# Router scores of a transformer layer: 32 small matmul groups moved from the normalisation loop to one batch behind it

## The reference

```python
xn = _layernorm(x, axis=-1)
x = x + attn(xn, Wq, Wk, Wv, Wo) + ffn(xn, router_w, bias, gate_w, up_w, down_w, sh_gate_w, sh_up_w, sh_down_w)
...
q = split_heads(x @ Wq.T); k = ...; v = ...          # 16 heads of 64
z = softmax(einsum('byq,byk->bkq', q, k) / sqrt(64))  # 64x64 per head, summed over the 4096 tokens
z = merge_heads(einsum('byz,bvy->bvz', z, v)) @ Wo.T
...
scores = sigmoid(x_flat @ router_w.T)                 # 16 experts
# best 2 of 4 groups, best 4 experts in them, weights normalised and times 2.5
routed = einsum('td,te->td', silu(x@gate)*(x@up) @ down, combine)
out = routed + shared experts (2 x 1024 wide)
```

## Time and profile before

| what | us |
|---|---|
| median of 2 runs (7301.42 to 7302.06) | 7301.74 |
| the profiled execution | 7300.52 |
| its span on the slowest core, core 7 | 7298.8 |
| spans of all cores | 7285.4 to 7298.8 |
| stage one, start of the span to the start of the softmax | 735.1 |

### The profile page before, as it was taken

How to read it: one execution, slowest core, us unless ns; L and a number is a source line. 1 busy time by engine, 2 the same in 40 slices (tenths; PEclk the granted TensorE clock), 3 DMA queues, 4 the chain that set the end, 5 groups by cost and what they waited for, 6 DMA issues and landing times.

```text
span 7298.8 us, 72612 instructions; the slowest of 8 cores (7285.4 to 7298.8 us)
## 1 busy us (share of the span) xinstructions
PE 6570.1 (90%) x30272; PEld 2954.1 (40%) x30272; DVE 1913.1 (26%) x3003; ACT 1469.9 (20%) x1905; POOL 170.6 (2%) x195
## 2 busy tenths in 40 slices
PE   1445777999999999999999999999999999999998
PEld 0222223444444444444444444444444444444443
DVE  1222442222222222222222222222222222222222
ACT  1110001222222222222222222222222222222221
POOL 0000000000000000000000000000000000000000
PEclk9778888999999999999999999999999999999999
DMA  5320222223222222222232432222222222222223
GB/s 100 62 48 22 72 92 55 46 35 45 37 42 40 35 35 35 35 35 35 35 45 37 67 55 42 37 45 35 35 35 35 35 35 35 41 41 40 42 36 57
DMA packets 275598, 323.53 MB, mean 44 GB/s; under 512 B 72496, under 2 KB 215856, under 8 KB 275280
## 3 DMA queue, kind: packets, MB, share of 16 engines
q0 software_dynamic: 193536, 251.70, 23.0%
q1 hardware_dynamic: 81744, 67.20, 3.5%
HBM read 503.42 MB, written 33.55 MB: 74 GB/s over the span
## 4 chain that ended last, share of the span: by engine, by line
PE 84%; DVE 3%; DMA 2%; issue 1%; DVEq 0%; SPq 0%; ACT 0%; POOLq 0%; POOL 0%; ACTq 0%
PE pheap L878 14%; PE pheap L808 14%; PE pheap L804 14%; PE pheap L881 14%; PE pheap L770 14%; PE pheap L774 14%; PE pheap L607 1%; DMA heap<-x 1%; DVE heap L817 1%; DVE heap L820 1%; DVE heap L631 1%; PE pheap L662 0%; DMA heap<-upw 0%; DVE heap L674 0%; DMA out<-heap 0%
## 5 line engine op out<-in xcount | busy, mean ns | idle before, releaser
L878 PE MATMUL pheap<-heap 128*128 128x512 bf16 x4608 | 1746.1, 379 | 124.1 <-DVE heap L820 124.1
L770 PE MATMUL pheap<-heap 128*128 128x512 bf16 x4608 | 1747.2, 379 | 29.8 <-DMA heap<-gatew 29.8
L783 ACT ACT_TABLE_LOAD x576 | 739.0, 1283 | 5137.1 <-PE pheap L774 5118.3
L804 PE MATMUL pheap<-heap 128*128 128x512 bf16 x4608 | 1748.8, 380 | 22.1 <-DVE heap L820 14.4
L808 PE MATMUL pheap<-heap 128*128 128x512 bf16 x4608 | 1748.7, 379 | 0.0
L774 PE MATMUL pheap<-heap 128*128 128x512 bf16 x4608 | 1747.2, 379 | 0.0
L881 PE MATMUL pheap<-heap 128*128 128x512 bf16 x4608 | 1746.2, 379 | 0.0
L817 DVE TENSOR_TENSOR heap<-pheap,heap 128x512 bf16<-128x512 f32 x576 | 398.4, 692 | 3244.1 <-PE pheap L808 3244.1
L902 DVE SCALAR_TENSOR_TENSOR heap<-pheap,heap 128x512 f32<-128x512 f32 x576 | 428.9, 745 | 1322.9 <-PE pheap L881 1322.9
L878 PEld LDWEIGHTS pheap<-heap 128*128 128x128 bf16 x4608 | 450.5, 98 | 692.8 <-issue 157.5
L770 PEld LDWEIGHTS pheap<-heap 128*128 128x128 bf16 x4608 | 451.1, 98 | 574.2 <-issue 31.1
(11 more groups left out here) (88 smaller groups left out, 1238.0 us busy)
## 6 DMA issues: line engine op xcount, KB each, us to landing
heap<-downw POOLq DMA_DIRECT2D x32, 2048.0 KB, 16.2
heap<-gatew POOLq DMA_DIRECT2D x62, 1024.0 KB, 11.3
heap<-upw POOLq DMA_DIRECT2D x62, 1024.0 KB, 15.7
heap<-x SPq DMA_DIRECT2D x64, 512.0 KB, 4.3
out<-heap SPq DMA_DIRECT2D x32, 512.0 KB, 2.9
out<-heap POOLq DMA_DIRECT2D x8, 2048.0 KB, 14.9
heap<-shg POOLq DMA_DIRECT2D x8, 1024.0 KB, 11.2
heap<-shu POOLq DMA_DIRECT2D x8, 1024.0 KB, 15.4
```

The costliest lines, as they stand in the source:

```text
L770: mm = t.matmul(bankf(0, 512), lhs, xnT[:, c * T + h * HALF + sa * 512: c * T + h * HALF + (sa + 1) * 512], start=(c == 0), stop=(c == 7))
L783: a = sc.activation(gfb[:, :], bankf(0, 512), AF.Silu, bias=f32(0.0), scale=f32(1.0))
L804: mm = t.matmul(bankf(1, 512), lhs, xnT[:, c * T + h * HALF + sa * 512: c * T + h * HALF + (sa + 1) * 512], start=(c == 0), stop=(c == 7))
L878: mm = t.matmul(bankf(bpar, 512), lhs, dwb[:, ft * D: ft * D + 512], start=(ft == 0), stop=(ft == 7))
```

## The change

The per-tile router work leaves the loop. Behind the last `emit_qk` a new loop over the tiles computes the 16 dot products of each tile, now in two PSUM banks in turn (3 and 7), and VectorE copies each 128x16 result into one 128x512 SBUF tile (`p3_em`). One Exp, one add and one reciprocal over the whole 128x512 follow. The buffers `p3_em`, `p3_tmp` and `p3_r16` belong to the routing decision and lie where the `x` tiles lay. `SCORES_DONE` is now the count after that reciprocal.

```diff
-                def p12_mm(t, i=i, par=par, sxtp=sxtp):
-                    sxtp.wait_at(t, rt_at[i])
-                    if i == 0:
-                        swt.wait_at(t, WQ_SWT)
-                    if i > 0:
-                        ssig.wait_at(t, score_at[i - 1])
-                    mm = None
-                    for c in range(8):
-                        mm = t.matmul(bankf(3, 16), xnT[:, c * T + i * P: c * T + (i + 1) * P],
-                                      rwT[:, c * 16:(c + 1) * 16],
-                                      start=(c == 0), stop=(c == 7))
-                    stt.inc(mm, 1)
-                block.tensor(p12_mm)
-
-                def p12_s3(sc, i=i):
-                    stt.wait(sc)
-                    if i > 0:
-                        sv.wait_at(sc, sxe_at[i - 1])
-                    ssig.inc(sc.activation(escore[:, :], bankf(3, 16),
-                                           AF.Exp, bias=f32(0.0), scale=f32(-1.0)), 1)
-                block.scalar(p12_s3)
-                score_at[i] = ssig.v
-
-                def p12_v3(v, i=i):
-                    ssig.wait_at(v, score_at[i])
-                    v.tensor_scalar(escore[:, :], escore[:, :], 1.0, None, ALU.add)
-                    v.drain()
-                    sv.inc(v.reciprocal(scores[:, 16 * i:16 * i + 16], escore[:, :]), 1)
-                block.vector(p12_v3)
-                sxe_at[i] = sv.v
...
             for k in range(NT - LAG, NT):
                 emit_qk(k)
+
+            for i in range(NT):
+                rb = 3 if i % 2 == 0 else 7
+
+                def p12_mm(t, i=i, rb=rb):
+                    if i == 0:
+                        sxt0.wait(t)
+                        sxt1.wait(t)
+                        swt.wait_at(t, WQ_SWT)
+                    if i >= 2:
+                        ssig.wait_at(t, ssig.v - 1)
+                    mm = None
+                    for c in range(8):
+                        mm = t.matmul(bankf(rb, 16), xnT[:, c * T + i * P: c * T + (i + 1) * P],
+                                      rwT[:, c * 16:(c + 1) * 16],
+                                      start=(c == 0), stop=(c == 7))
+                    stt.inc(mm, 1)
+                block.tensor(p12_mm)
+
+                def p12_lc(v, i=i, rb=rb):
+                    stt.wait(v)
+                    ssig.inc(v.tensor_copy(p3_em[:, 16 * i:16 * i + 16], bankf(rb, 16)), 1)
+                block.vector(p12_lc)
+
+            def p12_sexp(sc):
+                ssig.wait(sc)
+                ssc.inc(sc.activation(p3_tmp[:, 0:NT * 16], p3_em[:, 0:NT * 16],
+                                      AF.Exp, bias=f32(0.0), scale=f32(-1.0)), 1)
+            block.scalar(p12_sexp)
+
+            def p12_srec(v):
+                ssc.wait(v)
+                v.tensor_scalar(p3_r16[:, :], p3_tmp[:, 0:NT * 16], 1.0, None, ALU.add)
+                v.drain()
+                sv.inc(v.reciprocal(scores[:, :], p3_r16[:, :]), 1)
+            block.vector(p12_srec)
+            SCORES_BATCH = sv.v
...
-        SCORES_DONE = sxe_at[NT - 1]
+        SCORES_DONE = SCORES_BATCH
```

## The result

The changed kernel is faster: its time is 0.9691 of the time before, with a 95% interval of 0.9668 to 0.9714. Its undisturbed executions took 7073.8 and 7077.2 us, the kernel before 7298.5 to 7302.3. The forecast was 7082 us, a ratio of 0.9699. In 11 of the 13 executions of the changed kernel, as in 6 of the 10 of the kernel before, at least one die ran at a lower TensorE clock, which the comparison leaves out and which puts the median of all executions (8165 us against 7568) outside the stated range of 7055 to 7127.

What follows compares the result with a forecast made beforehand. Stage one was taken as bound by TensorE waiting in its router group for the newest tile (20.43 us a period). Savings 18.0 + 210.4 + 10.0 - 12.8 - 6.1 = 219.5 gave 7082 us, range 7055 to 7127.

Steps and rivals of the forecast that it cites:

- first copies: Start of the copies out of the first projections in stage one: forecast at 140.0 us instead of 157.97, 18.0 saved.
- sigmoid: One table load, Exp, add and reciprocal over 512 columns at the end of stage one: 6.1 us, all on the path.
- What bounds the kernel: Stage one's loop: a 20.43 us chain without overlap, TensorE held by the newest tile's router group; floor 10.25 us.
- The period that comes next: Stage-one loop without the router group: the x tiles' load, statistics and normalisation set 10.5 us a period.
- The interruptions: Wv transposes, Wo transposes and Wo staging in the stage-one loop, hidden by slack until now: together 29.6 us.
- Tiles 23 to 31: Last eight steps of stage one: 8 x 10.25 = 82.0 us against 92.0 before, 10.0 saved.
- The batch: 32 router groups alone behind the last copies, 0.4 us each with two banks: 12.8 us, upper end 24.3.
- The rule weighed: Ln and Exp share one table set, so all but L335's first load should go; prediction kept 1.28 us each period.
- The lower-clock rival: Stage-one loop: TensorE runs half of each period at 1.2 GHz, period 12.3 us, 41 us back, 7123 us; chance 0.09.
- The slow loads of x: Stage-one loop: denser x loads beside the transposes slow down, period 13.5 us, 69 us more, 7151 us; chance 0.05.
- The slower case: Stage three: denser stage one lowers its granted clock; from 6.1% of matmuls at 1.2 GHz, over 2% slower; chance 0.02.

## Where the prediction held, and which of its steps failed

The mechanism held, and so did the number wherever the cores kept their clock: 7073.8 and 7077.2 us, and 7082.5 in a repeat, against 7082. Two kinds of step failed: terms inside the sum were mis-sized, and the clock of one execution was taken for that of all. By the prediction's own steps, on core 2:

| point | before | forecast | measured |
|---|---|---|---|
| first copies | 157.97 | 140.0 | 138.7 |
| copies of tile 23 | 639.4 | 411.1 | 408.6 |
| copies of tile 31 | 731.5 | 493.1 | 490.6 |
| batch | | 12.8 | 12.4 |
| sigmoid | | 6.1 | 6.0 |

(The column of before is core 7, on which the prediction worked; its stage one was 0.7 us shorter than that of core 2.)

- *What bounds the kernel* was right, and it is shown, not only argued: with the router's wait left on TensorE and all else gone the period stayed at 20.5 us, and with all else left and only the order changed it fell to 10.25. One clause was wrong: the 8.1 us of reciprocals did not lie in the chain, since with them gone the period was still 20.54.
- *The period that comes next* was mis-sized: 10.5 against 10.25. The term that failed is the issue of a load to its statistics, taken as 4.67 us. It was 65.26 - 61.19 = 4.07, from rows shown above. The 4.67 row had been read behind eight transposes. With 4.07 the loop of the x tiles is 9.9 us and lies under TensorE's 10.25, not over it. Over 23 periods that is 5.8 us too much.
- *The interruptions* were taken at 29.6 us and came to 23.3 (18.6, 18.0 and 17.5 us between copies, less 10.25 each), another 6.3 too much. The step that failed is the overlap. The stops were sized about right: 21.95, 17.98 and 20.81 us passed between two statistics, 30.0 beyond three periods. But the forecast let them fall on the copies in full, and VectorE had been waiting 3.28 us for TensorE ahead of its copies. Behind the Wv and the Wo transposes that wait is gone, and the copies lose 3.4 us less than the statistics each time. The first of them:

```profile
227.65 0.69 DVE L326 BATCH_NORM_STATS2 heap<-heap 128x6 f32<-128x512 f32 x1
235.33 0.69 DVE L299 CAST heap<-pheap 128x512 bf16<-128x512 f32 x1 [3.28 <-PE pheap L291]
249.60 0.69 DVE L326 BATCH_NORM_STATS2 heap<-heap 128x6 f32<-128x512 f32 x1 [11.79 <-DMA heap<-x]
253.92 0.68 DVE L299 CAST heap<-pheap 128x512 bf16<-128x512 f32 x1
```

- *What was missing*: behind two of the interruptions, and in the first two periods, TensorE ran part of a period at the lower clock. Five periods of 11.7 to 13.2 us cost 10.9 us. I had put it at nothing in the sum and left it as a rival for all periods or none. The three errors nearly cancel (5.8 + 6.3 - 10.9 = 1.2). That the interval between first copies and tile 23 was met, 269.9 against 271.1, is luck: its parts were off by 5.8, 6.3 and 10.9 us.
- *Tiles 23 to 31*: 82.0 forecast, 490.6 - 408.6 = 82.0 measured.
- *The batch* overlapped as assumed, at 12.4 us. The 0.1 us of a release stood in no row. With one bank a group takes 0.77 us and a copy 0.17, which leaves 0.60 for the matmuls and two releases. The other bound was measured too: 24.5 us against the 24.3 stated.
- *The rule weighed*: 32 table loads are left at L335. The Trainium skill's rule (ScalarE: Activation LUTs, section "Table sets: the hidden batching unit") does not describe this kernel; the row of L783 did. And the table load cost nothing in the steady period, since 10.25 is not its loop.

```profile
L335 ACT ACT_TABLE_LOAD x32 | 41.1, 1283 | 358.0 <-DVE heap L329 358.0
L435 ACT ACT_TABLE_LOAD x1 | 1.3, 1283 | 90.9 <-DVE heap L430 90.9
```

- *The lower-clock rival* got 0.09 for every period of the loop. As a rule it was refuted (15 of 23 periods at 10.25 us). But two cores of another kernel, in one execution, had 15 long periods in a row at 2.4 us each, where the rival had 1.8, and cores 6 and 7 of the changed kernel had no period at 10.25. All four were granted 0.81 there. My argument against it, that the 2.74 us idle behind the loop leave no room for it, holds only for the clock at which those rows were read.
- *The slow loads of x* did not come: from issue to landing a load took 4.0 us in the median, 3.8 before.
- *The slower case* had 0.02, on the ground that stage three runs at a granted clock of 1.00. That is the step that failed for the median of all executions (8165 us). On cores 0 to 3 of the profiled execution stage three has its 1.00 and its length. Cores 4 to 7 were granted 0.81 for a part of it, and their spans are 7601.5 to 7667.9 us. Nothing ties this to the change, since the kernel before shows it too. But the forecast took the clock of one execution for that of all and had no term for another. What grants the lower clock stays open.

## What to carry to other kernels

On an engine that works in program order, a small group that waits for the newest data holds everything behind it, so its price is not its 0.36 us but the whole latency of the data it waits for. Put it behind work that is ready, with the same delay as that work: this gave the gain with nothing batched, and 18 us more than the batch in the median core. When such a wait goes, work out at once the loops that come next (here 10.25 and 9.9 us) and the interruptions that the old slack hid; here these were worth another 22 us by one load issued earlier at three places. And charge a stop to the path only with what exceeds the wait that it hides behind.

## What was not expected of the hardware

```profile
1500.00:2000.00 500.00, 489.85 (x1840) 203.61 (x1876) 103.81 (x154) 94.73 (x120) 10.48 (x12) 0.81 0.19 30
```

```profile
1500.00:2000.00 500.00, 489.96 (x2267) 221.14 (x2265) 126.99 (x189) 113.68 (x144) 13.11 (x15) 1.00 0.24 38
```

Core 7 is as core 6 and core 5 as core 4. From 5500 to 6500 us it is the other way round, 0.81 on cores 4 and 5 and 1.00 on 6 and 7.
- While a weight matrix is staged by GpSimd's queue, an x tile comes about 8 us later: from the issue of its load to the statistics 12.1, 12.4 and 12.0 us passed under the Wk, Wv and Wo stagings, against 4.07 alone. The mean DMA share in the 50 us around the last was 0.66, but 0.88 from 255 to 270 us, so full DMA engines are not ruled out as the reason.
